# Window attention: row scores as one piece of four row groups, V moved to the front of a step, K between the turn of the maximum and its use

## The reference

```
x: (4, 128, 112, 112)
xn  = (g - mean(g)) / sqrt(var(g) + 1e-5)           # 32 groups of 4 channels
xs  = roll(xn, (-3, -3), axis=(-2, -1))
qkv = einsum('bchw,oc->bohw', xs, w_qkv) + b_qkv
# q, k, v: windows of 49 tokens, 8 heads of 16 channels
scores = einsum('bxyhqd,bxyhkd->bxyhqk', q, k) / 4
out = einsum('bxyhqk,bxyhkd->bxyhqd', softmax(scores), v)
result = x + roll(out, (3, 3), axis=(-2, -1))
```

## Time and profile before

| | |
|---|---|
| median of 3 runs (lowest, highest) | 1022.41 us (1020.85, 1024.33) |
| profiled execution: time, span | 1024.01 us, 1022.1 us |
| mean granted TensorE clock | 0.985 |
| PE matmul busy | 967.7 us, 95% |
| PE weight loads busy | 764.0 us, 75% |
| DVE busy | 793.8 us, 78% |
| ACT busy | 696.6 us, 68% |
| POOL busy | 596.4 us, 58% |

### The profile page before, as it was taken

How to read it: one execution, slowest core, us unless ns; L and a number is a source line. 1 busy time by engine, 2 the same in 40 slices (tenths; PEclk the granted TensorE clock), 3 DMA queues, 4 the chain that set the end, 5 groups by cost and what they waited for, 6 DMA issues and landing times. The chain is left out here.

```text
span 1022.1 us, 104511 instructions
## 1 busy us (share of the span) xinstructions
PE 967.7 (95%) x46595; PEld 764.0 (75%) x46595; DVE 793.8 (78%) x1532; ACT 696.6 (68%) x1297; POOL 596.4 (58%) x1067
## 2 busy tenths in 40 slices
PE   0589999999999999999999999999999999999985
PEld 0367777777778777777778787777778777777764
DVE  6667888888888888888888888888877777777762
ACT  1447777777777777777777777777777777777752
POOL 1345665666666566666656665666666566666641
PEclk9979999999999999999999999999999999999995
DMA  9301101111111111111111000000000000000000
GB/s 381 131 4 63 63 31 63 63 49 45 63 63 33 61 63 57 37 63 63 40 55 47 32 16 31 31 31 16 32 31 16 31 31 31 16 31 31 19 31 35
DMA packets 29920, 51.96 MB, mean 51 GB/s; under 512 B 3650, under 2 KB 28868, under 8 KB 29764
## 3 DMA queue, kind: packets, MB, share of 16 engines
q1 hardware_dynamic: 29892, 51.59, 14.3%
HBM read 25.89 MB, written 25.69 MB: 50 GB/s over the span
## 5 line engine op out<-in xcount | busy, mean ns | idle before, releaser
L573 DVE TENSOR_REDUCE neg_max<-psum 100x16 f32<-100x784 f32 x256 | 249.4, 974 | 159.8 <-PE psum L730 159.8
L373 ACT ACTIVATE probs_t<-psum,exp_scale 128x800 f32<-128x800 f32 x256 | 237.3, 927 | 82.1 <-PE psum L747 52.8
L283 POOL TENSOR_SCALAR k_hi<-k 128x392 f16<-128x392 f32 x128 | 67.8, 530 | 230.2 <-PE psum L747 228.1
L730 PE MATMUL psum<-k_hi,q_masks 32*128 32x49 f16 x8192 | 197.5, 179 | 1.1 <-issue 0.6
L747 PE MATMUL psum<-q_masks,k_hi 32*64 32x100 f16 x8192 | 187.7, 207 | 3.3 <-issue 3.3
L305 POOL TENSOR_TENSOR stage<-mixed,image 128x343 f32 (+7 forms) x256 | 160.9, 650 | 43.5 <-issue 32.3
L730 PEld LDWEIGHTS psum<-k_hi,q_masks 32*128 32x128 f16 x8192 | 174.9, 91 | 10.9 <-issue 0.7
L730 PE MATMUL psum<-k_lo,q_masks 32*128 32x49 f16 x4096 | 182.2, 179 | 0.0
L566 DVE TENSOR_SCALAR q_masks<-q_halves,even_odd 128x800 f16<-128x800 f16 x256 | 171.6, 710 | 0.1
L747 PEld LDWEIGHTS psum<-q_masks,k_hi 32*64 32x64 f16 x8192 | 151.6, 105 | 26.4 <-issue 4.1
L730 PEld LDWEIGHTS psum<-k_lo,q_masks 32*128 32x128 f16 x4096 | 160.6, 91 | 0.0
(11 more groups left out here) (120 smaller groups left out, 1881.8 us busy)
## 6 DMA issues: line engine op xcount, KB each, us to landing
out_dram<-stage SPq DMA_DIRECT2D x64, 224.0 KB, 2.0
out_dram<-stage SPq DMA_DIRECT2D x64, 168.0 KB, 1.9
image<-in_x_dram SPq DMA_DIRECT2D x32, 224.0 KB, 2.6
image<-in_x_dram SPq DMA_DIRECT2D x1, 6104.0 KB, 27.3
image<-in_x_dram SPq DMA_DIRECT2D x34, 168.0 KB, 2.5
image<-in_x_dram SPq DMA_DIRECT2D x6, 896.0 KB, 9.7
image<-in_x_dram SPq DMA_DIRECT2D x1, 728.0 KB, 14.1
w_nat<-in_L_conv_w_qkv_dram SPq DMA_DIRECT2D x1, 192.0 KB, 2.4
```

The costliest lines, as they stand in the source:

```text
L373: nc.scalar.activation(probs_t[:, 2 * u:2 * u + 2, :, :].rearrange("p h a q -> p h (a q)"), psum[:, COL_BANKS, 0:PAIRS * ROWS2], ACT.Exp, ...
L573: nc.vector.tensor_reduce(neg_max[:, par, 2 * j:2 * j + 2, :], psum[0:ROWS2, ROW_BANKS, 0:GT] .rearrange("p h (w k) -> p h w k", k=TOK), A ...
L730: last = nc.tensor.matmul(psum[:, ROW_BANKS.start + h - 2 * j, w * TOK:(w + 1) * TOK], q_masks[rows, par, low + w * ROWS2:low + w * ROWS2 ...
```

## The change

- `row_scores` is one call a step. It goes over all four row groups for each window and term, into four banks: 6 and 7 for h = 0 and 1, 0 and 1 for h = 2 and 3. It waits for both maxima of the group before, and, as banks 6 and 7 are also the weighing's, for `join` of group g-2. `weigh` in turn waits for the first maximum.
- TensorE's `step` has V first. The first half of the key scores comes before `turn_max`, and `project_k` between `turn_max` and the use of the maximum.
- VectorE's `step` has `scale_rows` ahead of both maxima, which follow each other.
- `weigh` puts the pairs of windows 128 columns apart, so that `join` is one instruction for both banks; `PLACE` orders the spread inverse in the same way. ScalarE's `high_inverse` and `evac_even` change places.

```diff
--- before.py
+++ after.py
@@ -105,4 +105,5 @@
         psum = ctx.enter_context(nc.psum_tensor("psum", [128, 8, 512], f32))
-        ROW_BANKS, COL_BANKS, OUT_BANKS = slice(0, 2), slice(2, 4), slice(6, 8)
+        ROW_BANKS, COL_BANKS, OUT_BANKS = (slice(6, 8), slice(0, 2)), slice(2, 4), slice(6, 8)
         NEG_BANK, SUM_BANK, QK_BANK, V_BANK, INV_BANK = 0, 3, 4, 5, 5
+        PLACE = [w // 2 + PAIRS * (w % 2) for w in range(GW)]
         SPARE_SUM = slice(PAIRS * ROWS2, PAIRS * ROWS2 + TOK)
@@ -124,3 +125,3 @@
         q_high, q_low, q_masked = sem("q_high"), sem("q_low"), sem("q_masked")
-        row_mm = [sem("row_mm_0"), sem("row_mm_1")]
+        row_mm = sem("row_mm")
         max_done = [sem("max_done_0"), sem("max_done_1")]
@@ -388,3 +389,3 @@
                 wait(act, join_done, g + 1)
-                even = psum[:, OUT_BANKS, 0:PAIRS * ROWS2].rearrange("p s (a e q) -> p s a e q", e=2, q=QP)[:, :, :, 0, 0:TOK]
+                even = psum[:, OUT_BANKS, :].rearrange("p s (a q) -> p s a q", a=PAIRS)[:, :, :, 0:TOK]
                 nc.scalar.activation(even_out[:, :, :, :], even, ACT.Identity, scale=v_scale[:, 0:1]).then_inc(even_done, 1)
@@ -397,4 +398,4 @@
                 if live(g - 2):
+                    high_inverse(g - 2)
                     evac_even(g - 2)
-                    high_inverse(g - 2)
                 if live(g - 1):
@@ -570,5 +571,5 @@
             def maximum(g, par, j):
-                dve.wait_ge(row_mm[j], g + 1)
+                dve.wait_ge(row_mm, g + 1)
                 wait(dve, neg_split, g - 1)
-                nc.vector.tensor_reduce(neg_max[:, par, 2 * j:2 * j + 2, :], psum[0:ROWS2, ROW_BANKS, 0:GT]
+                nc.vector.tensor_reduce(neg_max[:, par, 2 * j:2 * j + 2, :], psum[0:ROWS2, ROW_BANKS[j], 0:GT]
                                         .rearrange("p h (w k) -> p h w k", k=TOK), AX.X, ALU.max, negate=True).then_inc(max_done[j], 1)
@@ -588,6 +589,5 @@
                 wait(dve, mixed_done, g + 1)
-                by_side = summed[:, :, :].rearrange("p (a s) q -> p s a q", s=2)
-                for s in range(2):
-                    odd = psum[:, OUT_BANKS.start + s, 0:PAIRS * ROWS2].rearrange("p (a e q) -> p a e q", e=2, q=QP)[:, :, 1, 0:TOK]
-                    last = nc.vector.scalar_tensor_tensor(by_side[:, s], odd, v_scale[:, 1:2], even_out[:, s, :, :], ALU.mult, ALU.add)
+                odd = psum[:, OUT_BANKS, :].rearrange("p s (a q) -> p (s a) q", a=PAIRS)[:, :, QP:QP + TOK]
+                last = nc.vector.scalar_tensor_tensor(summed[:, :, :], odd, v_scale[:, 1:2], even_out[:, :, :, :].rearrange("p s a q -> p (s a) q"),
+                                                      ALU.mult, ALU.add)
                 last.then_inc(join_done, 1)
@@ -598,4 +598,5 @@
                 wait(dve, add_done, g - 1)
-                nc.vector.tensor_tensor(mixed[:, par, :, :].rearrange("p w q -> p (w q)"), psum[:, INV_BANK, 0:GT],
-                                        summed[:, :, :].rearrange("p w q -> p (w q)"), ALU.mult).then_inc(mixed_done, 1)
+                nc.vector.tensor_tensor(mixed[:, par, :, :].rearrange("p (a s) q -> p s a q", s=2),
+                                        psum[:, INV_BANK, 0:GT].rearrange("p (s a q) -> p s a q", s=2, q=TOK),
+                                        summed[:, :, :].rearrange("p (s a) q -> p s a q", s=2), ALU.mult).then_inc(mixed_done, 1)
 
@@ -617,11 +618,10 @@
                     before()
+                for chunk in chunks:
+                    take_stats(image_at + chunk * STAT, chunk)
+                if live(g - 2):
+                    scale_rows(g - 2, par)
+                if after:
+                    after()
                 if live(g):
                     maximum(g, par, 0)
-                for chunk in chunks:
-                    take_stats(image_at + chunk * STAT, chunk)
-                if after:
-                    after()
-                if live(g - 2):
-                    scale_rows(g - 2, par)
-                if live(g):
                     maximum(g, par, 1)
@@ -719,16 +719,15 @@
 
-            def row_scores(g, par, j):
-
-                if j == 0:
-                    pe.wait_ge(q_masked, g + 1)
-                    pe.wait_ge(k_split, g + 1)
-                wait(pe, max_done[1 - j], g + j)
+            def row_scores(g, par):
+                pe.wait_ge(q_masked, g + 1)
+                pe.wait_ge(k_split, g + 1)
+                wait(pe, max_done[1], g)
+                wait(pe, join_done, g)
                 for w in range(GW):
                     for n, (low, k) in enumerate(((0, k_hi), (0, k_lo), (Q_LEN, k_hi))):
-                        for h in (2 * j, 2 * j + 1):
+                        for h in range(HP):
                             rows = slice(h * PC, (h + 1) * PC)
-                            last = nc.tensor.matmul(psum[:, ROW_BANKS.start + h - 2 * j, w * TOK:(w + 1) * TOK],
+                            last = nc.tensor.matmul(psum[:, ROW_BANKS[h // 2].start + h % 2, w * TOK:(w + 1) * TOK],
                                                     q_masks[rows, par, low + w * ROWS2:low + w * ROWS2 + 128], k[rows, par, w, 0:TOK],
                                                     start=n == 0, stop=n == 2, skip_group_check=True)
-                last.then_inc(row_mm[j], 1)
+                last.then_inc(row_mm, 1)
 
@@ -760,4 +759,4 @@
 
-            def column_scores(g, par, u):
-                if u == 0:
+            def column_scores(g, par, u, begin=False):
+                if begin:
                     wait(pe, exp_done[1], g)
@@ -765,2 +764,4 @@
                     scores_of_keys(g, par, u, True)
+                    return
+                if u == 0:
                     pe.wait_ge(neg_ready, g + 1)
@@ -787,2 +788,3 @@
                 pe.wait_ge(v_evac, g + 1)
+                pe.wait_ge(max_done[0], min(g + 2, GROUPS) if isinstance(g, int) else g + 2)
                 wait(pe, join_done, g + 1)
@@ -793,3 +795,3 @@
                             side = slice(PITCH * s, PITCH * (s + 1))
-                            last = nc.tensor.matmul(psum[c * PC:(c + 1) * PC, OUT_BANKS.start + s, a * ROWS2:(a + 1) * ROWS2],
+                            last = nc.tensor.matmul(psum[c * PC:(c + 1) * PC, OUT_BANKS.start + s, a * C:a * C + ROWS2],
                                                     v_rows[side, par, a, c * PC:(c + 1) * PC], probs_t[side, c, a, :],
@@ -805,3 +807,3 @@
                 for w in range(GW):
-                    last = nc.tensor.matmul(psum[:, INV_BANK, w * TOK:(w + 1) * TOK], pick_head[:, w, :], inv_rows[:, :],
+                    last = nc.tensor.matmul(psum[:, INV_BANK, PLACE[w] * TOK:(PLACE[w] + 1) * TOK], pick_head[:, w, :], inv_rows[:, :],
                                             start=True, stop=True, skip_group_check=True)
@@ -811,2 +813,4 @@
 
+                if live(g):
+                    project_v(g, par)
                 if live(g - 2):
@@ -814,11 +818,5 @@
                     weigh(g - 2, par)
-                if live(g):
-                    project_v(g, par)
                 if live(g - 1):
+                    column_scores(g - 1, 1 - par, 0, True)
                     turn_max(g - 1)
-                    column_scores(g - 1, 1 - par, 0)
-                if live(g):
-                    row_scores(g, par, 0)
-                if live(g - 2):
-                    spread_inverse(g - 2, live(g))
                 if live(g + 1):
@@ -826,5 +824,9 @@
                 if live(g - 1):
+                    column_scores(g - 1, 1 - par, 0)
+                if live(g):
+                    row_scores(g, par)
+                if live(g - 2):
+                    spread_inverse(g - 2, live(g))
+                if live(g - 1):
                     column_scores(g - 1, 1 - par, 1)
-                if live(g):
-                    row_scores(g, par, 1)
                 if live(g + 1):
```

## The result

| | before | after |
|---|---|---|
| median (lowest, highest), same chip | 1021.63 us (1018.97, 1024.33) | 1098.38 us (1097.22, 1099.89) |
| runs | 4 | 4 |
| ratio, 95% interval | | 1.0752 [1.0718, 1.0786] |
| profiled execution: time, span | 1024.01, 1022.1 us | 1097.22, 1095.4 us |
| mean granted TensorE clock | 0.985 | 0.939 |

The account below looks back on a forecast made before the run. TensorE's own stream was taken as the limit, 7.43 us a step. 126 x (7.43 - 6.98) = 56.7, less 8 for images, is 48.7: from 1024.0 to 975.3, less 1.6 to the median, 974 us; range 956 to 1010.

Parts of the forecast that it names:

- changes of image: VectorE's statistics between scale_rows and the next reciprocal, formerly free, would cost 2.7 us an image (between 1.3 and 3.9), 8 us for three.
- What is late next: DVE's join: Row scores now wait for VectorE's join: TensorE would wait 0 to 0.34 us, giving steps of 6.90 to 7.06, 6.98 taken.
- The masks are the uncertain part: VectorE's two masks of q, ahead of the join: 0.66 us with nothing on GpSimd, 1.42 beside its add.
- toss-up: Masks at 2.31 and GpSimd's add at 2.35 after V's start: either could go first; the middle, a 6.98 step, was taken.
- Add first: Case at the join: low_inverse at 3.77, join 3.95, released 4.61 after V's start; TensorE waits 0.34, step 7.06.
- Rival 3: GpSimd's add always wins against the masks: step 7.06, 12 us for images, 988 us, or 994 with more handovers; chance 0.13.
- The row scores' round: Four matmuls in four row groups would take 25 ns a round, 24 rounds 0.60 us, the stage 0.69 with its exit.
- rival 2: Row scores' four row groups share partly: 33 ns a round, row scores 0.80, step 7.09, 988 us; chance 0.12.
- PE's list: Sum of TensorE's stages in one step if nothing were late: 6.72 us, 0.71 under before.
- the floor by exp of 6.90: The second less-maximum stage waits for the first exp, until 5.45 after V's start, so a step takes at least 6.90 us.
- the covers by V and K: V first covers the second exp, at no cost; K covers the copy of the turned maximum, else 0.4 us would show.
- rival 4: The masks always go ahead of GpSimd's add: 6.90 a step, 4 us for the images, 960 us; chance 0.12.

Follow-up runs that it names:

- e7: The changed kernel with 40 useless small TensorE matmuls put ahead of the wait for the join in odd steps; 1049.32 us.
- e2: The changed kernel with GpSimd's add of the image ahead of its split of the maximum instead of behind it; 986.23 us.
- e8: The changed kernel with GpSimd's add of the image and its xn_lo each cut to one window of eight, most output left out; 969.33 us.
- e10: e2 with the statistics of a change of image moved into VectorE's idle time ahead of scale_rows; 960.26 us.
- e14: e10 with weight loads of 100 instead of 128 columns in two of three rounds of the row scores; 981.5 us, one run.

## Why the prediction was wrong

Where the time is, against the forecast of 974: 126 steps x (7.54 - 6.98) = 71; the falling clock 46 to 49; the changes of image 3.9 each instead of 2.7, 4 more; 121 to 124 together, of the distance 1098.4 - 974 = 124. Against before: 126 x (7.54 - 7.43) = 14, the clock's 46 to 49, and 12 for the images: 72 to 75 of the 77. The rest is not accounted for.

- **The step that failed: "What is late next: DVE's join".** "The masks are the uncertain part" was the error, three times over.
  - (a) It called the order of masks and add a toss-up, from masks at 2.31 and the add at 2.35 after V. The masks came at 2.34 (704.46 to 706.80), the add at 2.11: it follows the split of k by 2.36 (704.21 to 706.57), where 2.56 was taken from before. So the add came first. (The prediction's own sum had slipped here too: the second key scores end at 6.90 - 0.52 = 6.38 and not 6.41, which puts the add at 2.32, level with the masks.)
  - (b) "Add first: low_inverse comes 1.47 after the add's start" took over the pattern of before; here `xn_hi` follows the add at once, and the second mask is held behind it too: 1.73 (706.57 to 708.30).
  - (c) The low half of the inverse was counted at 0.18 to the join, on no other row than one in which nothing held it. It met `xn_lo` and took 0.91: join 0.83 after its start.
  - The join took its 0.61, and PE started 0.15 behind its end (709.74 to 709.89), where 0.05 was taken. So the row scores start at 2.11 + 1.73 + 0.83 + 0.61 + 0.15 = 5.43 and not at 4.61. The bound from above of this term, 0.34 of waiting, was an estimate of one meeting with one holder; measured is 1.16 in odd steps (5.43 - 4.27) and 0.13 in even ones.
  - The Trainium skill (SBUF — State Buffer, "Who interferes with whom") says that a VectorE instruction with two SBUF inputs, as the low half of the inverse has, collides with a GpSimd instruction that reads SBUF, and whichever is issued second waits for the end of the other. The traces agree: 0.26 alone, 0.91 behind `xn_lo`, while the join, with one input in PSUM, takes 0.61 to 0.63 beside `xn_hi` or `xn_lo`. The masks have one tensor and a factor for each partition as inputs, and they are held too, 0.66 alone and 1.58 behind the add and `xn_hi`. Asked of each VectorE instruction between the sums and the join, and not of the masks alone, the question what GpSimd has under way would have put a second wait into the sum.
- **A term that was missing: the clock.** The prediction priced each microsecond of PE's wait at itself. Idle times of 1.0 us ahead of the row scores were followed by 1.2 GHz in 28 places, and the falls cost 46 to 49 us. Against before that is the largest part of the 77: without it the change would still have been slower, by some 28 us (e7), so the late join alone was enough to make the forecast wrong. Rival 3, "the add always wins", had the right place, but gave 7.06 a step, 0.16 over exp's 6.90 where 0.64 was measured, and knew nothing of the clock, so it too came out faster than before.
- **The row scores' round.** 25 ns was right for the first 8 or 9 rounds of 24; the stage is 0.86, not 0.69, which is rival 2 (0.80) in size. Its price is small: with 0.86 PE's list is 6.72 + 0.17 = 6.89, no more than the 6.90 that exp gives anyway.
- **Changes of image.** The mechanism held: steps 8.58, 8.24, 9.04 and 8.20, VectorE without idle time from `scale_rows` on. In e7, where the clock is up, they are 8.50, 8.23, 8.97, 8.21: 33.9 less 4 x 7.51 = 3.9 an image, the upper end that the prediction gave.
- **What was right.** PE's stages, each to 0.02 apart from the row scores; the floor by exp of 6.90 (6.91 in e2, e8 and e10); the covers by V and K; the gain by four row groups; that steps with a timely join give some 960 (rival 4). That e10 meets this number so closely, 960.3, is in part luck: rival 4 had 4 us for the images in it, and e10 has none.

## What to carry to other kernels

A change that makes PE wait for a chain on VectorE has to be checked instruction by instruction for what GpSimd has under way at that moment, not for the one instruction that was seen held before: the short ones are held as long as the long ones. When TensorE's idle time grows from nothing to a microsecond a step, look at the strip of the granted clock first, and try a filling of useless matmuls: it tells the price of the clock from the price of the wait, if the steps at the full clock are compared too. And when a change that should gain loses, moving an unhurried step of a third engine may bring the gain back: here one GpSimd step was worth 112 us (1098.4 to 986.2).

## What was not expected of the hardware

- PE with records over 88% of the span lost the full clock 33 times; 28 of the falls came 1.5 to 2.4 us after an idle time of 1.0 us, and lasted 3.4 us each. 29 other idle times of 1.0 us had no fall behind them.
- A load of 100 columns of weights beside three others is slower than one of all 128: 47 ns a round against 25 (e14, one run, in every step).
- Four row groups run at 25 ns a round of eight instructions for 7 to 9 rounds, then at 33, whether 25 or 49 columns are streamed.
- VectorE's instruction of 49 elements took 0.26, 0.52, 0.91 or 1.01 us; in each of the longer cases it ended within 0.1 us of GpSimd's instruction beside it.
